# Taking score tiles and value tiles in pairs on TensorE in an adjacency-masked attention kernel

## The reference

```python
h = jnp.maximum(_layernorm(x), 0.0)
q = h @ Wq.T + bq
k = key @ Wk.T + bk
v = value @ Wv.T + bv
scores = jnp.einsum('nd,md->nm', q, k) / 64.0          # 4096 x 4096
adj_scores = scores * adj
adj_scores = jnp.where(jnp.abs(adj_scores) < 1e-05, -1e9, adj_scores)
prob = jax.nn.softmax(adj_scores, axis=-1)
out = x + (jnp.einsum('nm,md->nd', prob, v) @ Wm.T + bm)
```

## Time and profile before

| | |
|---|---|
| median of 3 runs | 1605.74 us (1605.52 to 1605.87) |
| time of the profiled execution | 1607.24 us |
| its span, first to last instruction | 1605.2 us |
| PE busy | 1569.5 us, 98% of the span |
| DVE busy | 993.6 us, 62% |
| ACT busy | 611.1 us, 38% |
| DMA queue of SP, share of 16 engines | 53.7% |
| mean granted TensorE clock | 0.994 of full |

### The profile page before, as it was taken

The page is one execution under the profiler, slowest core; times in us unless marked ns, Lnnn a source line. Parts: engine busy times, 40 slices in busy tenths (PEclk is TensorE's granted clock), DMA queues, the critical chain, the costliest instruction groups (busy, mean ns, idle before and its releaser), DMA issues.

```text
span 1605.2 us, 23476 instructions
## 1 busy us (share of the span) xinstructions
PE 1569.5 (98%) x7190; PEld 715.2 (45%) x7190; DVE 993.6 (62%) x2320; ACT 611.1 (38%) x963; POOL 105.0 (7%) x180
## 2 busy tenths in 40 slices
PE   7898999999999999999999999999999999999997
PEld 3543344444444444444444444444444444444442
DVE  4778765666666666666665665666566566666551
ACT  4666433333333333333333333333333333333331
POOL 0113100000000000000000000000000000000000
PEclk9999999999999999999999999999999999999999
DMA  9724455555555555555455555555645555455543
GB/s 348 248 59 93 112 121 122 132 125 118 123 127 122 119 136 119 120 123 130 118 117 138 120 122 125 129 118 117 138 118 128 121 124 123 117 132 124 119 100 83
DMA packets 431199, 205.72 MB, mean 128 GB/s; under 512 B 376128, under 2 KB 376128, under 8 KB 431040
## 3 DMA queue, kind: packets, MB, share of 16 engines
q1 hardware_dynamic: 430592, 205.07, 53.7%
q10 hardware_dynamic: 576, 0.27, 0.1%
HBM read 105.13 MB, written 8.39 MB: 71 GB/s over the span
## 4 chain that ended last, share of the span: by engine, by line
PE 92%; DVE 3%; DMA 2%; ACT 1%; issue 1%; POOL 0%; SPq 0%; DVEq 0%; ACTq 0%
PE R L506 13%; PE R L508 13%; PE R L507 13%; PE S L506 13%; PE S L507 13%; PE S L508 13%; PE M L506 3%; PE M L508 3%; PE M L507 3%; DMA pT<-ph 1%; PE R L574 1%; DMA ho<-row 1%; PE R L585 1%; ACT Vbuf L828 0%; PE R L618 0%
## 5 line engine op out<-in xcount | busy, mean ns | idle before, releaser
L855 ACT ACTIVATE drop<-Zbuf 128x512 f32<-128x512 f32 x256 | 161.1, 629 | 819.1 <-DVE cmx L1139 819.1
L1130 DVE SCALAR_TENSOR_TENSOR Zbuf<-S,rs,adjb 128x512 f32<-128x512 f32 x256 | 192.1, 750 | 349.2 <-PE S L508 344.7
L506 PE MATMUL R<-Vbuf,pT 128*128 128x512 f16 x1024 | 390.1, 381 | 13.1 <-POOL Vbuf L493 7.7
L508 PE MATMUL R<-Vbuf,pT 128*128 128x512 f16 x1024 | 390.1, 381 | 0.0
L507 PE MATMUL R<-Vbuf,pT 128*128 128x512 f16 x1024 | 389.9, 381 | 0.0
L506 PE MATMUL S<-Kbuf,qT 128*128 128x512 f16 x1024 | 388.2, 379 | 0.0
L507 PE MATMUL S<-Kbuf,qT 128*128 128x512 f16 x1024 | 388.1, 379 | 0.0
L508 PE MATMUL S<-Kbuf,qT 128*128 128x512 f16 x1024 | 388.1, 379 | 0.0
L1139 DVE CUSTOM_DVE_ANT_0 Zbuf<-drop,Zbuf 128x512 f32<-128x512 f32 x256 | 175.7, 686 | 0.0
L506 PEld LDWEIGHTS R<-Vbuf,pT 128*128 128x128 f16 x1024 | 100.5, 98 | 138.9 <-issue 14.4
L1188 DVE TENSOR_SCALAR drop<-drop,rs 128x512 f32<-128x512 f32 x256 | 140.9, 550 | 34.6 <-ACT drop L855 34.2
(11 more groups left out here) (165 smaller groups left out, 1161.5 us busy)
## 6 DMA issues: line engine op xcount, KB each, us to landing
adjb<-in_adj_dram SPq DMA_DIRECT2D x256, 256.0 KB, 2.8
xq<-in_x_dram SPq DMA_DIRECT2D x32, 256.0 KB, 2.8
Kbuf<-in_L_gnn_key_dram SPq DMA_DIRECT2D x8, 1024.0 KB, 14.3
xr<-in_x_dram SPq DMA_DIRECT2D x32, 256.0 KB, 2.7
out_dram<-xr SPq DMA_DIRECT2D x32, 256.0 KB, 2.3
Vbuf<-in_L_gnn_value_dram SPq DMA_DIRECT2D x7, 1024.0 KB, 8.5
pT<-ph SPq DMA_TRANSPOSE x132, 3.1
pT<-osb SPq DMA_TRANSPOSE x124, 3.1
```

Source lines behind the costliest of these rows:

```text
L506: nc.tensor.matmul(ps, lhs[0], rhs[0], start=start, stop=False)
L508: return nc.tensor.matmul(ps, lhs[1], rhs[0], start=False, stop=stop)
L855: nc.scalar.activation(drop[:, :], Zbuf[:, s.p, s.c * CW:(s.c + 1) * CW], ACT.Abs).then_inc(abs_ready, 1)
L1130: nc.vector.scalar_tensor_tensor(out=z, in0=S[s.j % 2][:, :], scalar=rs[:, r, 3, s.c // 2:s.c // 2 + 1], in1=adjb[:, s.j % ADJ_SLOTS, :], ...
```

## The change

Only TensorE's own order changes; no instruction is added or taken away, and no other engine's code is touched. `step` is cut into `scores`, `beginning` and `values`. From step 32 (`PAIRED`, the first of pass 2) to step 255 an even step takes its own score tile and that of the next step, and an odd step takes the value tile of the step before it and its own. What stands at the end of a step (`project_q` at c=3, the output at c=6) stays there. In steps 0 to 31, and from 256 on, the order is as it was.

```diff
+        PAIRED = FIRST * PASS
...
-            def step(s):
+            def scores(s):
                 if s.has_scores:
...
+            def beginning(s):
                 if isinstance(s.t, int):
...
+            def values(s):
                 if s.has_V:
...
+            def step(s):
+                if isinstance(s.t, int) and not PAIRED <= s.t < STEPS:
+                    scores(s)
+                    beginning(s)
+                    values(s)
+                elif s.j % 2 == 0:
+                    scores(s)
+                    scores(Step(s.i, s.j + 1))
+                else:
+                    values(Step(s.i, s.j - 1))
+                    values(s)
                 if s.pc == 3 and s.has_prep:
```

More of the change, by code:

```diff
@@ L284, in __init__ @@
                 self.t, self.j, self.c, self.p = PASS * i + j, j, j % NC, (j // NC) % 2
-                self.b = 2 * i + j // NC
+                self.b, self.i = 2 * i + j // NC, i
                 fixed = isinstance(i, int)
```

## The result

The changed kernel takes 1705.09 us (median of 4 runs, 1704.09 to 1706.70), the kernel before 1605.80 us (4 runs). The ratio is 1.0619, 95% interval 1.0603 to 1.0635: slower by 99.3 us. Forecast were 1704 us, with a range of 1669 to 1724, and slower. Its cause is not known, and it is left out of that kernel's ratio.

A forecast was written before the change was run, and what follows sets the result against it. PE, busy 98% of the span, was taken as the bound. Wait 68, half clock 31 and end 1 us sum to 100, giving 1706 against the median of 1605.7; 1704 us was forecast, range 1669 to 1724.

The forecast's parts named there:

- What bounds the kernel: Loop on TensorE: number of matmuls times spacing sets the time; joining like tiles saves nothing.
- The place: Before `project_q`: its rows' transposition queues on SP behind the probabilities', held by V(2); PE stops there, 27 times.
- The wait's size: In front of the projection: 2.5 us on the mean per block, 27 times, 68 us (63 to 76).
- The clock: Behind the projection's idle times: half clock in two of three blocks, 1.7 us each, 31 us (0 to 46).
- What was hidden: Score tiles, probabilities, output product and high part of the queries: later or closer in places, but no wait of PE.
- The output product: After V(4): its rows come a tile later but stay hidden, with 2.4 us to spare (5.0 before).
- The end: Turn from paired to single steps at V(243): one more idle time of 0.7 us, 1 us allowed in all.

The follow-up runs named there:

- three pairs of four: Changed kernel with steps c=2 and c=3 of every block back in the old order, the other six steps paired: 1607.29 us, ratio 1.0005.
- all four: Changed kernel with the rows' transposition issued ahead of the probabilities' in SP's step c=2, from step 32 on: 1606.13 us, ratio 1.0006.
- doing it alone: Changed kernel with only steps c=2 and c=3 paired, all others in the old order: 1705.50 us, ratio 1.0620.
- the filled kernel: Changed kernel with 11 matmuls that compute nothing used before each of the 27 late projections: 1674.44 us, ratio 1.0427.
- the four traces: Changed kernel with projection 6 matmuls later, 3 later, as changed, 3 earlier: 1636.40, 1656.95, 1705.09, 1731.78 us.

## Why the prediction was right

**What bounds the kernel.** PE did, and that is why pairing gains nothing: freed of its side effect it gives a ratio of 1.0005 (three pairs of four) and 1.0006 (all four), so the boundaries between like and unlike tiles cost the same, as one row of before had it.

**The place.** Shown by undoing it alone, by doing it alone, and by the order of SP's queue. The forecast wait for the rows was there 27 times, and no other.

**The wait's size.** 2.5 us each from start to start were forecast, and 2.44 measured (2.27 of idle and 0.17 that the matmuls' overlap hides); 5.27 us from V(2) to the projection in the block shown, against 5.40 in the block of before. The 27 make 66 us, where 68 were forecast. The stretch from V(2)'s end to SP's issue (0.20 and 0.21 us) and the landing (3.2 us at the median) were the same as before, as assumed.

One reading was a little off. The prediction took the 5.40 us as what the chain needs, and so found no slack. In the block of before the last matmul of V(3) starts at 834.35, and the projection starts one ordinary spacing later, in its slot:

```profile
834.35 0.38 PE L508 MATMUL R<-Vbuf,pT 128*128 128x512 f16 x1
834.57 0.38 PE L506 MATMUL M<-A_sb,ho 128*128 128x512 f16 x1
```

So the 5.40 are what the matmuls between give; the chain was done with the weight load at 834.43, 5.26 us after V(2)'s last matmul. In the changed kernel that load comes again 5.26 us after it, and the projection follows at once:

```profile
577.70 0.10 PEld L507 LDWEIGHTS M<-A_sb,ho 128*128 128x128 f16 x1 [2.79 <-DMA ho<-row]
```

There was some 0.15 us of slack, which is what 2.59 lacks to the 2.44 measured. The prediction allowed for it by taking 2.5.

**The clock.** Two in three were forecast to lose it, and 19 of 27 did, at 1.7 us each: 32 us, where 31 were forecast. That share was a choice between rows at 1.76 us and at 2.78 us, no more. That it came so close was luck, and with it the closeness of 1704 to 1705.1. What the rows did carry was that both ends were possible, and that the price is 1.7 us. The Trainium skill (TensorE: Matmul & The Clock Gate, section Why this matters for your kernels) warns only of longer gaps; by it the 30.7 us that the filled kernel recovered would not exist. Here idle times of 2.1 to 2.7 us were enough in 19 blocks of 27.

**What was hidden.** The output product kept its slack: in the block shown its transposition is issued at 591.59, and its first matmul starts at 597.53, 5.9 us later where 3.1 are needed, so 2.8 us against the 2.4 worked out. One wait I had missed: ACT's high part of the output rows waits for the landing of the projection's rows, since both use the tile `row`. In the block shown it sat idle 4.50 us for that (to 577.68), although V(2), the last value tile of its block, was done at 572.82. So the output rows were made only after the landing. It cost nothing, because they are transposed only behind V(4), from 591.59 on.

**The end.** 1 us was allowed for the turn to single steps. PE has one idle time more in the drain, 0.7 us (five where there were four).

## What to carry to other kernels

Where the busiest engine is full, look at a reordering not for what it joins but for what each moved piece released: here a value tile freed a slot, the slot held a transfer, and behind that transfer in the same in-order queue stood one that had nothing to do with it. If a chain of waits already ends exactly when it is needed, as the weight loads that waited 0.2 us showed, a delay of its start comes out nearly in full, once per block: here 2.44 us of 2.59.

The cheapest cure is in the queue: issue what is ready ahead of what waits. And a stall of TensorE of 2.1 us and more had a second price here, the half clock behind it. If the stall can't be removed, filling it with matmuls gives that part back (31 us of 99), and moving real ones into it gives more: with six of them only 30 us of the 99 were left.

## What the runs showed of the hardware

Of the idle times between 2.1 and 2.7 us some drop the granted clock to half, for about 3.4 us each time, and some don't. By the four traces the share is 0 of 27 at 1.0 us, 0 of 27 at 1.6 us (a few are possible in runs without a trace), 19 of 27 at 2.3 us and 27 of 27 at 2.9 us. The length alone does not decide: one of 2.71 us left the clock at 1.00, one of 2.13 us did not.

Nor does the fall follow the restart at a fixed distance. In the changed kernel it comes 0.2 to 1.3 us after the matmuls have begun again; in the kernel with the projection 3 matmuls earlier it comes in 21 of 27 blocks 0.1 to 0.4 us before that, while PE still stands. In the changed kernel the blocks that kept the clock come every third or fourth. Between two of them the fall comes later from block to block: 0.17, 0.67 and 1.09 us behind the restarts at 476.22, 526.93 and 577.71, then none behind the one at 628.50, then 0.18, 0.70 and 1.14 us. This looks as if what decides were where in time an idle stretch falls. That was not tested by itself: no run shifts the idle times and leaves their length alone. Since the length also sets the period of a block, the shares above need not hold for another kernel.
